# Attention stage of a two-layer gated cross-attention kernel: one power for both norms, aggregate instructions for variances, and a new order of work on every engine

## The chip, the cores and the metric

The kernel runs on one core of one Trainium2 chip. The time is the device time of one execution in microseconds (us). Engines are named as in the profile: PE is TensorE, DVE VectorE, ACT ScalarE, POOL GpSimd, SP the engine that issues the DMAs. Each engine takes its instructions in program order and waits for others by semaphores.

## The reference, cut to what matters

```
x = x + tanh(g_xattn[0]) * retention(layernorm(x), ctx, ctx, Wh, wg, wo, gn_gamma, gn_beta)
x = x + tanh(g_ffn[0]) * bit_ffn(layernorm(x), w1, w2, gamma)
x = x + tanh(g_xattn[1]) * long_conv(ctx, ctx, layernorm(x), ssm_kernel, D, 8)
x = x + tanh(g_ffn[1]) * experts(layernorm(x), ...)

retention:  O = einsum('hst,bthe->bshe', A, V)          # A from scores summed over the batch
            Y = (O - mean) / sqrt(var + 1e-3) * gn_gamma + gn_beta
            return relu(x @ wg) * Y @ wo
layernorm:  (x - mean) / sqrt(var + 1e-5)
bit_ffn:    x = x * rsqrt(mean(x * x) + 1e-6) * gamma
            xq = clip(round(x * s)) / s,  s = 127 / max(max|x|, 1e-5)     # per row, and so for h
            h = gelu(xq @ ternary(w1).T);  return hq @ ternary(w2).T
```

x is 16 x 256 rows of 512; the hidden width of bit_ffn is 2048. The change touches the first two lines' second half: from O to the end of bit_ffn.

## The kernel before

The program has four blocks that run one behind the other: setup, scores (queries, keys, gates and values of all chunks, the sum over the batch, the ternary weights), attention (`attn_block`), and experts. Only `attn_block` changes. It works on 8 chunks (NCH) of 512 rows, each in 4 tiles (j = 0 to 3) of 128 rows. In the text c or q is the chunk.

For a chunk the steps, by the names of the helper functions, are:

- `load_v`, `load_gate`, `load_x` (SP): the chunk's values into `stage`, its gates into `agate`, its rows of x into one of the two halves of `ax`.
- `cut_v` (ACT, then POOL): v into a high and a low part, 2048 columns each.
- `retention(q, s)`, s = 0 and 1 (PE): 24 matmuls of 256 columns into `ps_o`, which has room for one half s; so the next waits for `group_norm` of the one before.
- `group_stats`, `group_shift` (DVE) around `group_pow` (POOL): variance, its power -1/2, the shift; then `group_norm` (ACT) writes `ao`.
- `turn_o(q, k)` (PE): 4 transposes each, into `ps_r` (two banks); `times_gamma` (ACT), `gated` (DVE), `cut_z` (ACT, then POOL): the gated values, in high and low parts.
- `project(q, j)` (PE): 12 matmuls of 512 columns into `ps_r`; `add_x` (DVE) adds x and takes the statistics of x1.
- `pair_variance`, `pair_rms`, `pair_shift` (DVE) with `layer_pow` (POOL), for a pair of tiles: the layer norm's power, then from it the mean square and the power of the rms norm, then scale and shift; `layer_norm` (ACT) writes `ay`, `times_gain` (POOL) multiplies by gamma, `pair_scale` (DVE) takes the maximum and the scales, `round_y` (ACT) and `pair_bf16` (DVE) round to whole numbers in bf16, `turn_y` (SP) is a transposing DMA into `ayqT`.
- `mm1(c, j)` (PE): 4 groups of 4 matmuls of 512 columns, into three banks `ps_h` in turn; `gelu` (ACT) empties a bank; `scale_h` (DVE), `round_h` (ACT), `to_bf16` (DVE): maximum, scale, rounding of h (2048 columns, two buffers); `turn_h` (SP): transposing DMA into `ahqT` (two buffers).
- `mm2(c, j)` (PE): 16 matmuls of 512 columns into the one bank `ps_y`; `residual` (DVE) adds it to x1 and frees the bank; `store` (SP).

All loops over chunks are unrolled in Python. The order on each engine is written out by hand: after a start-up for chunk 0, the body of chunk c runs the ffn half of c (mm1 from tile 1, mm2, gelu, ...) with the retention half of q = c + 1 put between, and ends with mm1(q, 0). `variance` (lines 59 to 70) is six small DVE instructions, called for two columns at a time.

Of the kernel before, what the change touches and what calls it, by code (L numbers as in the profile page):

```python
# [468 lines left out]
def attn_block(nc, ctx, dram, keep):  # L469
# [23 lines left out]
    ostats, omom = sb("aostats", [P, 2, 6]), sb("aomom", [P, 5, 2])  # L493
    ove, orstd, oshift = (sb(n, [P, 2]) for n in ("aove", "aorstd", "aoshift"))
    stats, mom = sb("astats", [P, TJ, 6]), sb("amom", [P, 5, TJ])
    ve, rstd, sq, r2in, r2, scale, shift, amax, qrec, qscale, dq1 = (
        sb("a" + n, [P, TJ]) for n in "ve rstd sq r2in r2 scale shift amax qrec qscale dq1".split())
    hmax, hrec, hscale, dq2 = (sb("a" + n, [P, TJ]) for n in "hmax hrec hscale dq2".split())
# [28 lines left out]

    block = st.enter_context(nc.Block())

    @block.sync  # L530
    def _(sp):
        def load_v(n):
            sp.wait_ge(vlo_done, START + n)
            sp.dma_start(keep["stage"][:], dram["vals"][n]).then_inc(v_in, 16)
# [27 lines left out]
        for n in range(2):  # L562
            if n == 0:
                sp.sem_inc(v_in, 16)
            else:
                load_v(n)
            load_x(n)
            load_gate(n)
        turn_y(0, 0)
        turn_y(0, 1)  # L570
        for c in range(NCH):
            q = c + 1
            if q + 1 < NCH:
                load_v(q + 1)
            turn_h(c, 0)
            store(c, 0)
            if q + 1 < NCH:
                load_gate(q + 1)
            turn_h(c, 1)
            turn_h(c, 2)  # L580
            store(c, 1)
            turn_h(c, 3)
            if q < NCH:
                turn_y(q, 0)
            store(c, 2)
            if q < NCH:
                turn_y(q, 1)
            store(c, 3)
            if q + 1 < NCH:
                load_x(q + 1)  # L590
# [3 lines left out]
    def _(pool):  # L594
# [12 lines left out]
        def layer_pow(q, a):  # L607
            pool.wait_ge(mom_done, 12 * q + 6 * a + 6)
# [15 lines left out]
        cut_v(0)  # L624
        for q in range(NCH):
            if q == 0:
                group_pow(0, 0)
            group_pow(q, 1)
            for k in range(KT):
                cut_z(q, k)  # L630
            if q + 1 < NCH:
                cut_v(q + 1)
# [1308 lines left out]
```

## Time and profile before

| | us |
|---|---|
| three runs | 2332.95, 2332.93, 2327.42 |
| median | 2332.93 |
| profiled execution | 2325.81 |
| its span, first to last instruction | 2324.0 |
| mean granted clock of TensorE | 0.944 |
| busy in the span: PE, DVE, ACT, POOL | 2017.0, 1546.4, 1017.7, 952.0 |

The span is what lies between the first and the last instruction of the profiled execution; its own time is 1.8 us longer. The attention stage begins near 259 us of the span and its last residual starts at 803.31; before it lie setup and scores, behind it the experts. A granted clock of 1 is 2.4 GHz, of 0.5 is 1.2 GHz; a mean between is a mixture of the two. A matmul's record is longer than its spacing from the next, since matmuls overlap in the engine.

### The profile page before, as it was taken

The page shows a single profiled execution, that of the slowest core. Times are in us where ns is not written, and L with a number is a line of the kernel's source. Part 1 is how long each engine was busy: PE and PEld are TensorE (multiplying, and loading weights), DVE is VectorE, ACT ScalarE, POOL GpSimd, SP SyncE. Part 2 cuts the span into 40 slices and gives each one's busy share as a digit, 9 for nine tenths or more (in the row PEclk, how much of TensorE's full clock was granted, in tenths as well). Part 3 has the DMA queues.
Part 4 walks back from the last instruction along what each step waited for, and adds up shares of the span by engine and source line. Part 5 has one row for each costly group of instructions (what it writes and reads, how often), then busy time and mean ns, then how long its engine had stood idle before and what let it go on. Part 6 is the DMA issues. An engine that isn't in the chain of part 4 may idle for free.

```text
span 2324.0 us, 30136 instructions
## 1 busy us (share of the span) xinstructions
PE 2017.0 (87%) x10162; PEld 1602.5 (69%) x10162; DVE 1546.4 (67%) x2487; ACT 1017.7 (44%) x1414; POOL 952.0 (41%) x775
## 2 busy tenths in 40 slices
PE   5999568887787545799899899899899899899998
PEld 4989444444454234688788788788788788688787
DVE  4776456666666358588578678678578579578511
ACT  3345345555555321633633633633633633443432
POOL 0110133333332021465465465465465465365464
PEclk9999779999999857899999999999999999899999
DMA  6666314443443321322332332332232242232231
GB/s 214 235 217 231 131 54 116 111 105 96 108 118 82 69 66 46 104 85 90 111 95 86 109 103 86 106 106 86 93 119 82 80 124 90 72 113 73 69 136 64
DMA packets 169968, 248.76 MB, mean 107 GB/s; under 512 B 91280, under 2 KB 92688, under 8 KB 163632
## 3 DMA queue, kind: packets, MB, share of 16 engines
q1 hardware_dynamic: 169616, 247.86, 34.3%
q8 instruction: 34, 0.56, 0.1%
q14 instruction: 30, 0.25, 0.0%
q10 hardware_dynamic: 288, 0.10, 0.0%
HBM read 193.26 MB, written 33.69 MB: 98 GB/s over the span
## 4 chain that ended last, share of the span: by engine, by line
PE 43%; DVE 7%; issue 6%; ACT 5%; POOL 3%; DMA 1%; ACTq 0%; SPq 0%; DVEq 0%; POOLq 0%
PE e_ps_u L54 4%; PE e_ps_u L56 4%; PE e_ps_u L55 4%; PE e_ps_m L54 4%; PE e_ps_m L56 3%; PE e_ps_m L55 3%; PE e_ps_out L54 3%; PE e_ps_out L55 3%; PE e_ps_out L56 3%; PE e_ps_g L56 3%; PE e_ps_g L55 3%; PE e_ps_g L54 3%; POOL e_dn_lo L1185 1%; DVE e_kv_lo L1504 1%; DVE e_x3T L1532 1%
## 5 line engine op out<-in xcount | busy, mean ns | idle before, releaser
L1180 POOL TENSOR_TENSOR e_gu_lo<-e_gu_raw,e_gu_hi 128x1024 fp32r<-128x1024 f32 (+1 forms) x128 | 272.8, 2131 | 449.6 <-ACT e_gu_hi L1269 447.3
L1532 DVE TENSOR_REDUCE e_x3T<-e_zp 128x128 f32<-128x1024 f32 x128 | 267.4, 2089 | 4.4
L54 PE MATMUL e_ps_u<-e_xn_hi,e_gu_hi 128*128 128x512 f32 x512 | 205.5, 401 | 4.0 <-DVE e_xn_lo L1554 2.5
L54 PE MATMUL e_ps_out<-e_hd_hi,e_dn_hi 128*128 128x512 f32 x512 | 208.8, 408 | 0.0
L54 PE MATMUL e_ps_m<-e_kv_hi,e_t_hi 128*128 128x288 f32 x592 | 180.7, 305 | 29.7 <-DVE e_kv_lo L1504 22.1
L55 PE MATMUL e_ps_out<-e_hd_lo,e_dn_hi 128*128 128x512 f32 x512 | 205.2, 401 | 0.0
L56 PE MATMUL e_ps_out<-e_hd_hi,e_dn_lo 128*128 128x512 f32 x512 | 205.2, 401 | 0.0
L55 PE MATMUL e_ps_u<-e_xn_lo,e_gu_hi 128*128 128x512 f32 x512 | 203.7, 398 | 0.0
L56 PE MATMUL e_ps_u<-e_xn_hi,e_gu_lo 128*128 128x512 f32 x512 | 203.6, 398 | 0.0
L958 PE MATMUL ps_h<-w1q,ayqT 128*128 128x512 bf16 x512 | 130.3, 403 | 79.4 <-ACT ah L681 71.9
L1203 POOL TENSOR_TENSOR e_kv_raw<-e_ke 128x512 f32<-128x512 f32 x128 | 139.4, 1089 | 125.7 <-DVE e_kv_lo L1504 95.5
L1185 POOL TENSOR_TENSOR e_dn_lo<-e_dn_raw,e_dn_hi 128x512 fp32r<-128x512 f32 x128 | 179.6, 1403 | 6.9 <-ACT e_dn_hi L1275 6.9
L1477 DVE TENSOR_TENSOR e_hd_lo<-e_hd,e_hd_hi 128x512 fp32r<-128x512 f32 x128 | 125.2, 978 | 78.6 <-ACT e_hd_hi L1297 78.6
L56 PE MATMUL e_ps_m<-e_kv_hi,e_t_lo 128*128 128x288 f32 x592 | 177.0, 299 | 0.0
L55 PE MATMUL e_ps_m<-e_kv_lo,e_t_hi 128*128 128x288 f32 x592 | 176.8, 299 | 0.0
L1283 ACT ACTIVATE e_sg<-e_ps_g,vecs 128x512 f32<-128x512 f32 x96 | 66.2, 690 | 242.4 <-PE e_ps_g L56 241.5
L1472 DVE SCALAR_TENSOR_TENSOR e_hd<-e_ps_u,vecs,e_sgw 128x512 f32<-128x512 f32 x96 | 71.7, 747 | 140.7 <-PE e_ps_u L56 116.0
L1297 ACT ACTIVATE e_hd_hi<-e_hd 128x512 fp32r<-128x512 f32 x128 | 80.4, 628 | 190.0 <-DVE e_hd L1472 189.7
L1194 POOL TENSOR_TENSOR e_sgw<-e_sg,e_wb 128x512 f32<-128x512 f32 x96 | 127.1, 1324 | 80.2 <-ACT e_sg L1283 79.5
L958 PEld LDWEIGHTS ps_h<-w1q,ayqT 128*128 128x128 bf16 x512 | 48.4, 101 | 151.1 <-ACT ah L681 87.5
L54 PE MATMUL e_ps_g<-e_xn_hi,e_gu_hi 128*128 128x512 f32 x384 | 152.5, 397 | 0.0
L56 PE MATMUL e_ps_g<-e_xn_hi,e_gu_lo 128*128 128x512 f32 x384 | 151.5, 395 | 0.0
(271 smaller groups left out, 5304.7 us busy)
## 6 DMA issues: line engine op xcount, KB each, us to landing
e_gu_raw<-in_mgu SPq DMA_DIRECT2D x96, 512.0 KB, 3.3
e_dn_raw<-in_md SPq DMA_DIRECT2D x128, 256.0 KB, 3.2
e_wb<-wts SPq DMA_DIRECT2D x8, 1536.0 KB, 6.6
stage<-in_x SPq DMA_DIRECT2D x8, 1024.0 KB, 6.8
c<-in_ctxT SPq DMA_DIRECT2D x8, 1024.0 KB, 5.8
raw_w<-in_w1T SPq DMA_DIRECT2D x8, 1024.0 KB, 4.8
raw_w<-in_w2T SPq DMA_DIRECT2D x8, 1024.0 KB, 7.3
gates<-gate SPq DMA_DIRECT2D x8, 1024.0 KB, 4.8
```

Of the source, the lines that this page charges most:

```text
L54: nc.tensor.matmul(out, w_hi, x_hi, start=first, stop=False, skip_group_check=skip)
L55: nc.tensor.matmul(out, w_hi, x_lo, start=False, stop=False, skip_group_check=skip)
L56: return nc.tensor.matmul(out, w_lo, x_hi, start=False, stop=last, skip_group_check=skip)
L958: last = nc.tensor.matmul(h_bank(c, j, n)[:], yqT[:, j, k], keep["w1q"][:, k, n * 512:(n + 1) * 512], start=(k == 0), stop=(k == KT - 1))
L1180: nc.gpsimd.tensor_tensor(gu_lo[:, s % 2, a], gu_raw[:, s % 2, a], f32(gu_hi[:, s % 2, a]), ALU.subtract).then_inc(gulo_done, 1)
L1185: nc.gpsimd.tensor_tensor(dn_lo[:, s % 2], dn_raw[:, s % 2], f32(dn_hi[:, s % 2]), ALU.subtract).then_inc(dnlo_done, 1)
L1194: nc.gpsimd.tensor_tensor(sgw[:], sg[:], wb[:, (s - SHARED) // 2], ALU.mult).then_inc(sgw_done, 1)
L1203: nc.gpsimd.tensor_tensor(out[:, :, 0:32].rearrange("p b (d i) -> p b d i", i=CD), view(ke, m * B * EXT, (EXT, B), (0, 4), (1, CD)), view( ...
L1297: nc.scalar.activation(hd_hi[:, s % 2], hd[:], ACT.Copy).then_inc(hdhi_done, 1)
L1472: nc.vector.scalar_tensor_tensor(out=hd[:], in0=ps_u[:], scalar=vecs[:, V_BU + e:V_BU + e + 1], in1=sgw[:], op0=ALU.add, op1=ALU.mult).the ...
L1477: nc.vector.tensor_tensor(hd_lo[:, s % 2], hd[:], f32(hd_hi[:, s % 2]), ALU.subtract).then_inc(hdlo_done, 1)
L1532: nc.vector.tensor_reduce(x3T[:, lb].rearrange("p (b n) -> p b n", b=B)[:, :, hh * CD:(hh + 1) * CD], zv(5, (1, 8), (21, 8)), AX.X, ALU.ad ...
```

## The change

The norm of x and the rms norm behind it become one power: with v the variance, the scale of both is (v (1 + 1e-6) + 1e-6 * 1e-5) ** -0.5, so `pair_rms`, the second power in `layer_pow` and the product in `pair_shift` go. Variances come from `bn_aggr` (one instruction a tile, mean and variance from the statistics) and one small instruction for the pair, instead of `variance`. In `pair_scale` and `scale_h` a factor 1/127 is merged into the maximum's step, one small instruction less in each.

The hand-written order of all five engines is replaced by a list per engine in which a loop variable i runs over shifted chunks: `at(op, c, ...)` issues the step if chunk c exists. The steps are finer: mm1 and gelu by group n, `layer_norm`, `round_y`, `times_gain` and `to_whole` (formerly `pair_bf16`) by tile. Waits that the old order made needless are added: `group_norm` of s = 0 behind the last chunk's `turn_o`, `layer_norm` behind `to_whole` of the chunk before, `pair_shift` behind its `layer_norm`, `dq1` behind the gelus of the chunk before.

The diff, cut: declarations, semaphore names, the deleted hand-written order (it stands in the listing above) and unchanged steps are left out.

```diff
+    def at(op, c, *which):

+        if 0 <= c < NCH:
+            op(c, *which)
...
+            if n == 0:
+                sp.sem_inc(v_in, 16)
+            else:
+                sp.wait_ge(vlo_done, START + n)
+                sp.dma_start(keep["stage"][:], dram["vals"][n]).then_inc(v_in, 16)
...
+        for i in range(-2, NCH + 2):
+            at(turn_h, i - 2, 2)
+            at(turn_h, i - 2, 3)
+            at(store, i - 2, 0)
+            at(turn_y, i - 1, 1)
+            at(store, i - 2, 1)
+            at(store, i - 2, 2)
+            at(load_x, i)
+            at(store, i - 2, 3)
+            at(turn_h, i - 1, 0)
+            at(load_v, i + 2)
+            at(load_gate, i + 1)
+            at(turn_h, i - 1, 1)
+            at(turn_y, i, 0)
...
-            nc.gpsimd.tensor_tensor(rstd[:, cols], ve[:, cols], mhalf[:, cols], ALU.pow).then_inc(rstd_done, 1)
-            pool.wait_ge(rms_step, 6 * q + 3 * a + 3)
-            nc.gpsimd.tensor_tensor(r2[:, cols], r2in[:, cols], mhalf[:, cols], ALU.pow).then_inc(r2_done, 1)
-
-        def times_gain(q, a):
-            for j in (2 * a, 2 * a + 1):
-                pool.wait_ge(y_done, 4 * q + j + 1)
-                nc.gpsimd.tensor_tensor(y[:, j], y[:, j], keep["gam"][:], ALU.mult).then_inc(yg_done, 1)
+            nc.gpsimd.tensor_tensor(scale[:, cols], ve[:, cols], mhalf[:, cols], ALU.pow).then_inc(scale_done, 1)

+        def times_gain(q, j):
...
+        for i in range(-2, NCH):
+            at(times_gain, i, 2)
+            at(group_pow, i + 1, 1)
+            at(times_gain, i, 3)
+            at(cut_v, i + 2)
+            for k in range(4):
+                at(cut_z, i + 1, k)
+            at(group_pow, i + 2, 0)
+            at(layer_pow, i + 1, 0)
+            at(times_gain, i + 1, 0)
+            at(times_gain, i + 1, 1)
+            at(layer_pow, i + 1, 1)
...
+            if q > 0 and s == 0:
+                act.wait_ge(oT_done, 4 * q)
...
+        def layer_norm(q, j):
+            act.wait_ge(shift_done, 2 * q + j // 2 + 1)
+            if q > 0:
+                act.wait_ge(yq_done, START + 4 * (q - 1) + j + 1)
+            nc.scalar.activation(y[:, j], x1(q)[:, j], ACT.Identity, bias=shift[:, j:j + 1], scale=scale[:, j:j + 1]).then_inc(y_done, 1)

+        def round_y(q, j):
...
+        for i in range(-3, NCH):
+            at(gelu, i, 0, 0)
+            at(group_norm, i + 1, 1)
+            for n in range(1, 4):
+                at(gelu, i, 0, n)
+            at(round_y, i, 2)
+            at(round_y, i, 3)
+            at(times_gamma, i + 1, 0)
+            at(times_gamma, i + 1, 1)
+            at(gelu, i, 1, 0)
+            at(round_h, i, 0)
+            at(cut_z, i + 1, 0)
+            at(times_gamma, i + 1, 2)
+            at(cut_z, i + 1, 1)
+            at(times_gamma, i + 1, 3)
+            at(gelu, i, 1, 1)
+            at(cut_z, i + 1, 2)
+            at(gelu, i, 1, 2)
+            at(cut_z, i + 1, 3)
+            at(gelu, i, 1, 3)
+            for n in range(4):
+                at(gelu, i, 2, n)
+            at(round_h, i, 1)
+            at(round_h, i, 2)
+            at(layer_norm, i + 1, 0)
+            at(layer_norm, i + 1, 1)
+            at(gelu, i, 3, 0)
+            at(group_norm, i + 2, 0)
+            at(gelu, i, 3, 1)
+            at(gelu, i, 3, 2)
+            at(round_y, i + 1, 0)
+            at(round_y, i + 1, 1)
+            at(gelu, i, 3, 3)
+            at(layer_norm, i + 1, 2)
+            at(layer_norm, i + 1, 3)
+            at(cut_v, i + 3)
+            at(round_h, i, 3)
...
-            variance(nc, dve, ostats, omom, ove[:], GN_EPS, omom_done, 12 * q + 6 * s)
+            for b in range(2):
+                nc.vector.bn_aggr(omv[:, b], ostats[:, b]).then_inc(omom_done, 1)
+            dve.wait_ge(omom_done, 6 * q + 3 * s + 2)
+            nc.vector.tensor_scalar(ove[:], omv[:, :, 1], GN_EPS, None, ALU.add).then_inc(omom_done, 1)
...
-            variance(nc, dve, stats[:, cols], mom[:, :, cols], ve[:, cols], LN_EPS, mom_done, 12 * q + 6 * a)
-
-        def pair_rms(q, a):
-
-            cols = slice(2 * a, 2 * a + 2)
-            n = 6 * q + 3 * a
-            dve.wait_ge(rstd_done, 2 * q + a + 1)
-            nc.vector.tensor_tensor(sq[:, cols], rstd[:, cols], rstd[:, cols], ALU.mult).then_inc(rms_step, 1)
-            dve.wait_ge(rms_step, n + 1)
-            nc.vector.scalar_tensor_tensor(out=r2in[:, cols], in0=ve[:, cols], scalar=LN_EPS, in1=sq[:, cols], op0=ALU.subtract,
-                                           op1=ALU.mult).then_inc(rms_step, 1)
-            dve.wait_ge(rms_step, n + 2)
-            nc.vector.tensor_scalar(r2in[:, cols], r2in[:, cols], RMS_EPS, None, ALU.add).then_inc(rms_step, 1)
...
+            for j in (2 * a, 2 * a + 1):
+                nc.vector.bn_aggr(mv[:, j], stats[:, j]).then_inc(mom_done, 1)
+            dve.wait_ge(mom_done, 6 * q + 3 * a + 2)
+            nc.vector.tensor_scalar(ve[:, cols], mv[:, cols, 1], 1.0 + RMS_EPS, RMS_EPS * LN_EPS, ALU.mult, ALU.add).then_inc(mom_done, 1)
...
-            dve.wait_ge(r2_done, 2 * q + a + 1)
-            nc.vector.tensor_tensor(scale[:, cols], rstd[:, cols], r2[:, cols], ALU.mult).then_inc(shift_done, 1)
-            dve.wait_ge(shift_done, 4 * q + 2 * a + 1)
-            nc.vector.scalar_tensor_tensor(out=shift[:, cols], in0=mom[:, 0, cols], scalar=-0.5, in1=scale[:, cols], op0=ALU.mult,
+            dve.wait_ge(scale_done, 2 * q + a + 1)
+            if q > 0:
+                dve.wait_ge(y_done, 4 * (q - 1) + 2 * a + 2)
+            nc.vector.scalar_tensor_tensor(out=shift[:, cols], in0=mv[:, cols, 0], scalar=-1.0, in1=scale[:, cols], op0=ALU.mult,
                                            op1=ALU.mult).then_inc(shift_done, 1)
...
-            nc.vector.tensor_scalar(amax[:, cols], amax[:, cols], 1e-5, None, ALU.max).then_inc(qs_done, 1)
+            nc.vector.tensor_scalar(step[:, cols], amax[:, cols], 1e-5, 1.0 / QMAX, ALU.max, ALU.mult).then_inc(qs_done, 1)
             dve.wait_ge(qs_done, n + 2)
-            nc.vector.reciprocal(qrec[:, cols], amax[:, cols]).then_inc(qs_done, 1)
-            nc.vector.tensor_scalar(dq1[:, cols], amax[:, cols], 1.0 / QMAX, keep["wmean"][:, 0:1], ALU.mult, ALU.mult).then_inc(qs_done, 2)
-            dve.wait_ge(qs_done, n + 5)
-            nc.vector.tensor_scalar(qscale[:, cols], qrec[:, cols], QMAX, None, ALU.mult).then_inc(qs_done, 1)
...
-            nc.vector.tensor_scalar(hmax[:, col], hmax[:, col], 1e-5, None, ALU.max).then_inc(hs_done, 1)
+            nc.vector.tensor_scalar(hstep[:, col], hmax[:, col], 1e-5, 1.0 / QMAX, ALU.max, ALU.mult).then_inc(hs_done, 1)
             dve.wait_ge(hs_done, n + 2)
-            nc.vector.reciprocal(hrec[:, col], hmax[:, col]).then_inc(hs_done, 1)
-            nc.vector.tensor_scalar(dq2[:, col], hmax[:, col], dq2w[:], None, ALU.mult).then_inc(hs_done, 1)
-            dve.wait_ge(hs_done, n + 4)
-            nc.vector.tensor_scalar(hscale[:, col], hrec[:, col], QMAX, None, ALU.mult).then_inc(hs_done, 1)
+            nc.vector.reciprocal(hscale[:, col], hstep[:, col]).then_inc(hs_done, 1)
+            nc.vector.tensor_scalar(dq2[:, col], hstep[:, col], dq2w[:], None, ALU.mult).then_inc(hs_done, 1)
...
+        for i in range(-2, NCH + 1):
+            at(pair_variance, i, 1)
+            at(residual, i - 1, 0)
+            at(to_whole, i, 0)
+            at(to_whole, i, 1)
+            at(pair_shift, i, 1)
+            at(scale_h, i - 1, 3)
+            at(group_stats, i + 1, 1)
+            at(residual, i - 1, 1)
+            at(group_shift, i + 1, 1)
+            at(to_bf16, i - 1, 3)
+            at(pair_scale, i, 1)
+            at(scale_h, i, 0)
+            at(residual, i - 1, 2)
+            at(gated, i + 1, 0)
+            at(to_whole, i, 2)
+            at(to_whole, i, 3)
+            at(gated, i + 1, 1)
+            at(to_bf16, i, 0)
+            at(gated, i + 1, 2)
+            at(gated, i + 1, 3)
+            at(residual, i - 1, 3)
+            at(group_stats, i + 2, 0)
+            at(scale_h, i, 1)
+            at(scale_h, i, 2)
+            at(add_x, i + 1, 0)
+            at(add_x, i + 1, 1)
+            at(group_shift, i + 2, 0)
+            at(pair_variance, i + 1, 0)
+            at(to_bf16, i, 1)
+            at(pair_shift, i + 1, 0)
+            at(to_bf16, i, 2)
+            at(add_x, i + 1, 2)
+            at(add_x, i + 1, 3)
+            at(pair_scale, i + 1, 0)
...
-                pe.wait_ge(x1_done, START + 4 * q)
+                pe.wait_ge(x1_done, START + 4 * q - 1 + k)
...
+        for i in range(-2, NCH + 1):
+            at(mm2, i - 1, 1)
+            for n in range(4):
+                at(mm1, i, 0, n)
+            at(mm2, i - 1, 2)
+            at(turn_o, i + 1, 0)
+            at(turn_o, i + 1, 1)
+            for n in range(3):
+                at(mm1, i, 1, n)
+            at(turn_o, i + 1, 2)
+            at(turn_o, i + 1, 3)
+            at(mm2, i - 1, 3)
+            at(retention, i + 2, 0)
+            at(mm1, i, 1, 3)
+            for n in range(4):
+                at(mm1, i, 2, n)
+            at(project, i + 1, 0)
+            at(project, i + 1, 1)
+            at(mm1, i, 3, 0)
+            at(mm1, i, 3, 1)
+            at(project, i + 1, 2)
+            at(project, i + 1, 3)
+            at(mm1, i, 3, 2)
+            at(mm2, i, 0)
+            at(mm1, i, 3, 3)
+            at(retention, i + 2, 1)
```

## Rows read from the trace of the kernel before

**Rows 1.** Windows view: span, length, busy of PE, PEld, DVE, ACT, POOL, clock.
```profile
546.00:607.00 61.00, 49.23 (x243) 29.79 (x242) 41.11 (x94) 33.20 (x41) 19.28 (x15) 0.97 0.43 112
...
900.00:1000.00 100.00, 70.05 (x349) 58.22 (x350) 64.45 (x110) 44.76 (x66) 36.26 (x33) 0.80 0.25 77
```

**Rows 2.** Waits in the attention stage (329 to 803): total, times, longest.
```profile
PE ps_h L958 <- ACT ah L681: 71.9, 31, 6.0
...
PE ps_y L966 <- DVE ax L843: 20.8, 15, 3.9
```

**Rows 3.** Timeline of TensorE (start, length): where mm1 of chunks 0, 1, 7 begins.
```profile
318.23 5.30 PE L958 MATMUL ps_h<-w1q,ayqT 128*128 128x512 bf16 x12 [7.25 <-DMA ayqT<-ayq]
...
386.60 2.75 PE L958 MATMUL ps_h<-w1q,ayqT 128*128 128x512 bf16 x12
...
756.36 2.75 PE L958 MATMUL ps_h<-w1q,ayqT 128*128 128x512 bf16 x12
```

**Rows 4.** Timeline of TensorE: matmuls of the four kinds at the full clock.
```profile
301.14 0.39 PE L54 MATMUL ps_r<-wo_hi,az_hi 128*128 128x512 f32 x1
...
307.94 0.28 PE L54 MATMUL ps_o<-av_hi,at_hi 128*128 128x256 f32 x1
...
310.70 0.28 PE L56 MATMUL ps_o<-av_hi,at_lo 128*128 128x256 f32 x1
...
346.61 3.62 PE L966 MATMUL ps_y<-w2q,ahqT 128*128 128x512 bf16 x16
...
350.06 2.75 PE L958 MATMUL ps_h<-w1q,ayqT 128*128 128x512 bf16 x12
```

**Rows 5.** Groups by line, 424.96 to 485.87: count, busy us, mean ns.
```profile
L681 ACT ACTIVATE ah<-ps_h,adq 128x512 f32<-128x512 f32 x16 | 10.2, 685 | 3.6 <-PE ps_h L958 3.5
...
L822 DVE TENSOR_REDUCE ahmax<-ah 128x1 f32<-128x2048 f32 x4 | 9.1, 2281 | 1.3 <-ACT ah L681 1.3
...
L686 ACT ACTIVATE ah<-ah,arnd,ahscale 128x2048 f32<-128x2048 f32 x4 | 8.3, 2087 | 0.0
...
L767 DVE SCALAR_TENSOR_TENSOR ax<-ps_r,gains,ax 128x512 f32<-128x512 f32 x5 | 3.7, 748 | 14.6 <-PE ps_r L56 14.5
```

**Rows 6.** Timeline of VectorE in the first chunk, the chain to the shift.
```profile
304.22 0.16 DVE L62 TENSOR_TENSOR amom<-astats 128x2 f32<-128x2 f32 x1
...
305.80 0.16 DVE L782 TENSOR_TENSOR asq<-arstd 128x2 f32<-128x2 f32 x1 [0.81 <-POOL arstd L610]
...
307.17 0.16 DVE L792 TENSOR_TENSOR ascale<-arstd,ar 128x2 f32<-128x2 f32 x1 [0.81 <-POOL ar L612]
...
311.03 1.22 DVE L802 TENSOR_REDUCE aamax<-ay 128x2 f32<-128x1024 f32 x1 [3.50 <-POOL ay L617]
```

**Rows 7.** Timeline of VectorE and GpSimd where both are at work.
```profile
446.85 2.50 POOL L617 TENSOR_TENSOR ay<-ay,gam 128x512 f32<-128x512 f32 x2 [1.32 <-ACT ay L670]
...
447.16 0.97 DVE L62 TENSOR_TENSOR aomom<-aostats 128x2 f32<-128x2 f32 x1
...
477.12 1.50 DVE L837 TENSOR_SCALAR ahq<-ah 128x2048 bf16<-128x2048 f32 x1
...
477.89 5.11 POOL L597 TENSOR_TENSOR av_lo<-stage,av_hi 128x2048 fp32r<-128x2048 f32 x1 [0.36 <-ACT av_hi L645]
```

**Rows 8.** Timeline where the stage starts and ends.
```profile
294.25 0.80 PE L54 MATMUL ps_r<-wo_hi,az_hi 128*128 128x512 f32 x1 [5.40 <-POOL az_lo L605]
...
785.06 1.89 PE L958 MATMUL ps_h<-w1q,ayqT 128*128 128x512 bf16 x4 [3.91 <-ACT ah L681]
...
803.31 0.75 DVE L843 SCALAR_TENSOR_TENSOR ax<-ps_y,adq,ax 128x512 f32<-128x512 f32 x1 [4.12 <-PE ps_y L966]
```

**Rows 9.** DMA issues 329 to 800: line, count, KB each, median us to landing.
```profile
ax<-in_x SPq DMA_DIRECT2D x6, 1024.0 KB, 5.7
...
ahqT<-ahq SPq DMA_TRANSPOSE x32, 4.3
...
ayqT<-ayq SPq DMA_TRANSPOSE x15, 3.1
```

More of the change, by code:

```diff
@@ L561, in _ @@
         sp.sem_inc(x2_out, START)
[L562 to L590, printed above, removed]
+        for i in range(-2, NCH + 2):
[12 more added lines that the diff above has]
+            at(turn_y, i, 0)
         sp.wait_ge(x2_out, START + 16 * TJ * NCH)
@@ L623, in _ @@
         pool.wait_ge(consts_done, 1)
[L624 to L632, printed above, removed]
-            for a in range(2):
-                layer_pow(q, a)
-                times_gain(q, a)
-            if q + 1 < NCH:
-                group_pow(q + 1, 0)
+        for i in range(-2, NCH):
[10 more added lines that the diff above has]
+            at(layer_pow, i + 1, 1)
     @block.scalar
@@ L808, in pair_scale @@
[L808 to L816 removed]
+            nc.vector.reciprocal(qscale[:, cols], step[:, cols]).then_inc(qs_done, 1)
@@ L949, in project, with mm1 @@
             last.then_inc(wo_done, 1)
-        def mm1(c, j):
-            pe.wait_ge(yT_in[j // 2], 16 * (c + 1))
-            for n in range(4):
-                if 16 * c + 4 * j + n >= HBANKS:
-                    pe.wait_ge(gelu_done, START + 16 * c + 4 * j + n - HBANKS + 1)
-                for k in range(KT):
-                    last = nc.tensor.matmul(h_bank(c, j, n)[:], yqT[:, j, k], keep["w1q"][:, k, n * 512:(n + 1) * 512],
-                                            start=(k == 0), stop=(k == KT - 1))
-                last.then_inc(h_done, 1)
+        def mm1(c, j, n):
+            if n == 0:
+                pe.wait_ge(yT_in[j // 2], 16 * (c + 1))
+            if 16 * c + 4 * j + n >= HBANKS:
+                pe.wait_ge(gelu_done, START + 16 * c + 4 * j + n - HBANKS + 1)
+            for k in range(KT):
+                last = nc.tensor.matmul(h_bank(c, j, n)[:], yqT[:, j, k], keep["w1q"][:, k, n * 512:(n + 1) * 512],
+                                        start=(k == 0), stop=(k == KT - 1))
+            last.then_inc(h_done, 1)
         def mm2(c, j):
@@ L969, in _ @@
         pe.sem_inc(mm2_done, START)
-        retention(0, 0)
-        retention(0, 1)
-        for k in range(KT):
-            turn_o(0, k)
-        for j in range(TJ):
-            project(0, j)
-        retention(1, 0)
-        mm1(0, 0)
-        for c in range(NCH):
-            q = c + 1
-            last = q == NCH
-            if not last:
-                retention(q, 1)
-            mm1(c, 1)
-            mm1(c, 2)
-            if not last:
-                for k in range(KT):
-                    turn_o(q, k)
-            mm2(c, 0)
-            mm1(c, 3)
-            if not last:
-                for j in range(TJ):
-                    project(q, j)
-            mm2(c, 1)
-            if q + 1 < NCH:
-                retention(q + 1, 0)
-            mm2(c, 2)
-            mm2(c, 3)
-            if not last:
-                mm1(q, 0)
+        for i in range(-2, NCH + 1):
[24 more added lines that the diff above has]
+            at(retention, i + 2, 1)
     st.close()
```

172 lines of the change are left out of this document (30 added, 142 removed).

## Prediction, made before the changed kernel was run

> **What bounds the kernel now.** I read five views, in this order. The busy time in windows of about one chunk (61 us) says which engine is nearest to its limit: TensorE is busy 49.2 us of 61, VectorE 41.1, ScalarE 33.2, GpSimd 19.3, at a granted clock of 0.97 [rows 1]. So no engine is full, and the time of the attention stage is made by waits. The view of who waited for whom, over the stage, says which: TensorE's first-layer matmuls `ps_h` stand 71.9 us behind ScalarE's gelu and its second-layer matmuls 20.8 us behind the residual (there is one bank `ps_y`) [rows 2]. A program in a fixed order on five queues waits in one place because the order of another puts something in front. The timeline of TensorE gives the length of a round, counted from mm1(c, 0) to mm1(c+1, 0): 318.23 to 386.60, 68.4 us, for the first, then (756.36 - 386.60) / 6 = 61.6, and 62.6 over all seven [rows 3]. The stage is some 545 of the 2324 us of the span; the setup and scores before it and the experts behind it (there the granted clock and the busy time are another matter [rows 1]) are not touched, and I carry them over unchanged.
>
> **What TensorE alone needs for a round.** At the full clock, 16 second-layer matmuls start 350.06 - 346.61 = 3.45 us after the 16 before, 0.216 each; mm1 has the same shape. 64 + 64 of them make 27.6. The projection's matmuls start (307.94 - 301.14) / 30 = 0.227 apart, 48 make 10.9; retention's (310.70 - 307.94) / 23 = 0.12, 48 make 5.8 [rows 4]. The 16 transposes at about that last rate make 1.9. The sum is 46.2 us. So a new order can take at most 62.6 - 46.2 = 16.4 from a round, times 7 = 115 us. The small arithmetic is not worth much by itself; whether that floor is reached is the question.
>
> **Small operations.** In the first chunk nothing hides the chain from the statistics to the shift: six variance steps and a power take 305.80 - 304.22 = 1.58 us, three steps and a second power 307.17 - 305.80 = 1.37, then two steps; a step is 0.16 busy [rows 6]. The change drops the second power with its three steps (1.37) and the product `scale` (0.2), and turns six variance steps into three (two bn_aggr, one add). No row shows a bn_aggr. Three small steps are 0.5 against at most 1.0 for six; from above, an instruction over 512 columns takes 0.75 [rows 5], and one over 6 no more: 2 x 0.75 + 0.16 = 1.66. So the variance moves by -0.5 to +0.7; I take -0.3, as a 6-column step is nearest to the small ones. The chain shortens by about 1.9 us, twice per chunk. VectorE loses 26 small instructions per chunk (24 variance steps become 12, six rms steps and two products go, six scalings are merged), 26 x 0.16 = 4.2: 41.1 - 4.2 = 37 us busy. GpSimd loses two powers of at most 1.37 - 3 x 0.16 = 0.9: 17.6 or more [rows 1, 6].
>
> **The new order, walked.** I put TensorE's new list at its floor, with 0 at mm2(i-1,1), and ask of each other engine whether it delivers in time, with durations from [rows 5]: gelu 0.69 (0.6 when they follow each other, the records overlap), round_h 2.09, cut_v as round_h (as many columns), scale_h 2.28 for the maximum and 0.4 for its steps, add_x 0.75 with 0.7 of statistics, to_bf16 1.2 (1.50 with a hold in it [rows 7]), other 512-column work 0.75.
> TensorE: mm2(i-1,1) 0 to 3.5, mm1(i,0) to 6.9, mm2(i-1,2) to 10.4, turn_o 0 and 1 to 11.4, mm1(i,1) three quarters to 14.0, turn_o 2 and 3 to 15.0, mm2(i-1,3) to 18.5, retention(i+2,0) to 21.4, mm1 to 25.7, project 0 and 1 to 31.1, mm1 to 32.8, project 2 and 3 to 38.3, mm1 39.1, mm2(i,0) 42.6, mm1 43.5, retention(i+2,1) 46.2.
> Then: gelu(i,2,3) ends at 26.5; scale_h(i,2) to 29.3; add_x 0 and 1 to 33.3; add_x 3 ends 40.0; pair_scale 41.7; round_y 43.1; residual(i,0) has to wait for mm2(i,0), 43.5; to_whole 44.3; the transpose of y lands 3.1 later [rows 9], at 47.5. mm1(i+1,0) is due at 46.2 + 3.5 = 49.7, so 2.2 us are spare. The same tail, from the maximum to the first matmul, took 318.23 - 311.03 = 7.2 us where nothing stood in it [rows 3, 6]; here it has 40.0 to 49.7. The late gelu(i,3,3), the cut of v behind retention(i+2,1), and round_h(i-1,3) end at 4.2 of the next round, and gelu(i,0,0) is due for mm1(i,0,3) at 6.0, spare about 1. The transposes of h land in 4.3 [rows 9] with over 10 us to spare in three cases of four; h(i-1,3) is the tight one, below.
> DMAs are queued on SP in the list's order. load_x(i+1) waits for residual(i-1,3), at about 22, and holds back store(i-1,3), turn_h(i,0) (due 39), load_v, load_gate and turn_h(i,1). The load lands in 5.7 [rows 9], at 28 to 29, and add_x(i+1,0) wants it at 29.3: just in time. If it is late, VectorE is held by the excess and project 2 still has some 3 us.
> So by the engines' order alone TensorE would hardly stop.
>
> **What the walk must add: GpSimd and VectorE in each other's way.** From 446.85 GpSimd multiplies two tiles in 2.50; a two-column add on VectorE, begun at 447.16, takes 0.97 instead of 0.16, until 448.13, when the first of the two is through. At 477.12 a to_bf16 begins and ends at 478.62; GpSimd's part of cut_v, begun at 477.89, takes 5.11, of which 4.4 lie behind that end [rows 7]. Before, cut_v fell where VectorE waited for the projection. The new lists put it (and times_gain 3) right behind group_pow, and VectorE then has group_shift (two inputs from SBUF), to_bf16(i-1,3) and pair_scale before it. group_shift at 4.4 gets in before cut_v at 4.6; to_bf16 then stands from 4.8 to about 9.4, pair_scale ends at 12.2 instead of 7.5, and round_y 2 and 3 hold ScalarE's times_gamma until 13.6. turn_o 2 starts at 14.4 instead of 14.0, and residual(i-1,2) and h(i-1,3)'s transpose come at 15.5 for an mm2 due at 15.0. From there VectorE catches up, waiting again for project 3. So a hold by cut_v is 4.4 to 5.1 long. It costs 4.6 us of VectorE and some 0.7 of TensorE. Between 0 (the waiting is hidden) and 4.6 (all of it reaches TensorE) I take 0.7. With 1.6 for ordinary lateness (load_x, handoffs, some matmuls at half clock after a gap) I set a round at 46.2 + 0.7 + 1.6 = **48.5 us**.
> The Trainium skill, page SBUF — State Buffer, section Who interferes with whom, says that VectorE with two SBUF inputs, or in a two-port mode, and GpSimd exclude each other for a whole instruction, whichever came first. By that rule the group_shift too stands 4.5 us if cut_v is first, so it speaks against this order, and the rival B below is what it would give. The trace agrees in the 0.97 us row.
>
> **Start and end.** Before the first round the new list puts retention(1,0) into the 5.4 us in which TensorE waited for `az_lo` [rows 8]. It is off the path, and the projection starts at the full clock: 14 matmuls save 0.2 each, 2.8. With the 1.9 of the chain that is 4.7. Against it, cut_v(1) now follows group_pow(0,1) on GpSimd directly, and group_shift(0,1) may stand for its 4.5 us. Bounds 0 and 4.5; I take half. So mm1(0,0) starts 2.4 earlier, at 315.8. The first round has the start-up in it: 51 instead of 68.4. At the end, from mm1(7,0) on, before took 803.31 + 0.75 - 756.36 = 47.7 [rows 3, 8]. The last gelu, scale, rounding, transpose, mm2 and residual, from the end of the last mm1 at 785.06 + 1.89, take 804.1 - 787.0 = 17 in both [rows 8]. In the new list the last mm1 is reached about 24.5 after mm1(7,0), so 41.5: 6 less.
>
> **The sum.** mm1(7,0) starts at 315.8 + 51 + 6 x 48.5 = 657.8 instead of 756.4: 98.6 less. With 6 at the end it is 105 less than the profiled execution of 2325.8, that is 2221. The median of the runs shown lies 7 us above that execution; I take half of this, 2224.
>
> **Rivals.**
> A, the floor: the waits vanish, rounds of 46.2 (49 the first), mm1(0,0) at 313.6. 313.6 + 49 + 277.2 = 639.8, 123 less with the end: 2203. It counts into the forecast and gives its low end.
> B, the holds are not absorbed: VectorE stands behind cut_v for 4.5 us and TensorE with it, each round. 48.5 + 4.5 = 53, 7 x 4.5 = 31 more: 2255. For it: the 0.97 us row [rows 7], and cut_v's place. Against it: VectorE has 46.2 - 37 = 9 us of room. Its far end is VectorE and GpSimd never at work together: 37 + 17.6 = 55 a round, 7 x (62.6 - 55) = 53 and 8 at the ends less, 2265 to 2272.
> C, the order changes nothing, and only the shorter chain counts: twice 1.9 per round, 7 x 3.8 = 27 and 8 at the ends: 2291 to 2298. The waits of TensorE for gelu [rows 2] would stay at 70 us. Against it: these waits are made by what the old list puts between gelus, and that is what is moved.
> D, slower: TensorE's waits become many and short instead of few, and the granted clock falls. In the window 900 to 1000 the clock is 0.80 with TensorE busy 70 us of 100 [rows 1], against 0.97 in the stage. The place is all of TensorE's list. A round then takes 46.2 / clock + 2.3; it passes 62.6 + 1.2 (what the ends save, per round) from a clock of 0.75 down, and at 0.70 it is 68.3, giving 2326 + 7 x 5.7 - 8 = 2358. Against it: the walk leaves no gap of more than about 1 us.
> E, none of it measurable: rounds of 62, 2320 to 2333.
>
> **Chances.** Forecast with A 0.67 (rounds of 46 to 51 us, 2200 to 2245), B 0.22, C 0.06, E 0.02, D 0.03. A range of 2200 to 2266 holds the first and nearly all of B. A measurement of this kernel can tell about 0.3% (7 us) from no change. Faster by more than that: 0.95; within 0.02; slower 0.03.
>
> **What would show it.** Right: mm1(c,0) starts 48 to 49 us apart; `ps_h` behind gelu falls from 71.9 to under 15; TensorE's clock at 0.98 or more; VectorE 37 busy per round; bn_aggr at 0.2 or less; mm1(0,0) near 316; 41 us from mm1(7,0) to the end. Wrong: to_bf16 or group_shift of 2 to 5 us beside cut_v in every round together with TensorE idle at mm2(·,3) or turn_o (B); waits of add_x for x; a landing of the y transpose over 5 us; a clock below 0.9 (D).

## The result and the profile after

| | before | after |
|---|---|---|
| median, us | 2332.66 | 2190.18 |
| lowest and highest of four runs | 2327.42, 2332.95 | 2189.53, 2191.32 |
| profiled execution | 2325.81 | 2189.84 |
| its span | 2324.0 | 2188.0 |
| last residual ends | 804.06 | 674.16 |
| from there to the end of the span | 1519.9 | 1513.8 |

The ratio after/before is 0.9395, with a 95% interval of 0.9378 to 0.9411. The change is faster, by 142 us; 2224 was forecast, and 2190.2 lies below the low end of the range, 2200.

The windows of the changed kernel (span, length, busy of PE, PEld, DVE, ACT, POOL with their instructions, granted clock, DMA share, GB/s) answer [rows 1]:

```profile
409.00:456.00 47.00, 47.00 (x246) 29.47 (x245) 41.30 (x70) 34.68 (x43) 21.69 (x14) 1.00 0.58 146
...
546.00:607.00 61.00, 61.00 (x319) 36.79 (x318) 52.92 (x87) 45.15 (x60) 24.67 (x16) 1.00 0.51 121
```

TensorE is busy 47.00 us of 47 and 61.00 of 61, at the full clock: in this stage it has become the bound. VectorE is busy 41.30 us of 47, which is 40.5 in a round of 46.1 and not 37 as forecast. The largest waits of TensorE from 320 to 660 answer [rows 2]:

```profile
PE ps_h L902 <- ACT ah L668: 2.2, 3, 1.2
PE ps_y L910 <- DMA ahqT<-ahq: 1.9, 1, 1.9
```

Of the 71.9 us behind gelu 2.2 are left. Of the 20.8 behind the residual none is left up to 660 and 0.8 in the last pass behind it. Now it is ScalarE that waits for TensorE: the same view for all engines has `ACT ah L668 <- PE ps_h L902: 24.0, 53, 2.2`. The timeline of TensorE has these starts of mm1 for chunks 0, 1, 6 and 7, against [rows 3]:

```profile
316.89 5.04 PE L902 MATMUL ps_h<-w1q,ayqT 128*128 128x512 bf16 x16 [4.83 <-DMA ayqT<-ayq]
...
361.07 0.59 PE L902 MATMUL ps_h<-w1q,ayqT 128*128 128x512 bf16 x2
...
591.64 0.38 PE L902 MATMUL ps_h<-w1q,ayqT 128*128 128x512 bf16 x1
...
632.92 0.60 PE L902 MATMUL ps_h<-w1q,ayqT 128*128 128x512 bf16 x2 [0.33 <-DMA ayqT<-ayq]
```

The first round takes 44.2 us (68.4 before), the next five (591.64 - 361.07) / 5 = 46.1 each (61.6), the last 41.3. The floor of the prediction was 46.2. From mm1(7,0) to the last residual, which starts at 673.41 and takes 0.75, it is 41.2 (47.7 before, [rows 8]).

VectorE in the first chunk, and then VectorE and GpSimd in a steady round, answer [rows 6] and [rows 7]:

```profile
304.57 0.25 DVE L757 BATCH_NORM_AGGREGATE amv<-astats 128x2 f32<-128x6 f32 x2
...
305.83 0.16 DVE L766 SCALAR_TENSOR_TENSOR ashift<-amv,ascale 128x2 f32<-128x2 f32 x1 [0.81 <-POOL ascale L602]
...
454.38 1.22 DVE L806 TENSOR_SCALAR ahq<-ah 128x2048 bf16<-128x2048 f32 x1
454.40 5.58 POOL L589 TENSOR_TENSOR av_lo<-stage,av_hi 128x2048 fp32r<-128x2048 f32 x1
...
456.75 3.25 DVE L776 TENSOR_SCALAR astep<-aamax 128x2 f32<-128x2 f32 x1
```

Two bn_aggr take 0.25 us together. The chain from the statistics to the shift's start is 305.83 - 304.57 = 1.3 us, against 304.22 to 307.37 before, so 1.9 shorter, as worked out. And GpSimd's part of cut_v does hold VectorE in each of the five rounds from 361 to 592: it is a scaling of two columns that stands 3.25 us for its usual 0.17. to_bf16, which was expected to be held, began 0.02 us ahead of cut_v and ran in 1.22, and it was cut_v that took 5.58 (4.5 where nothing stands in its way).

### The profile page after: what moved, and what is told of

Its sections match the earlier page's. It is cut to its first block, busy times and chain, and to the rows that moved or that the text cites. A ratio compares the mean times of both kernels' runs of the same rounds, so it can differ in the third digit from the quotient of the medians.

```text
span 2188.0 us, 30039 instructions
## 1 busy us (share of the span) xinstructions
PE 1979.3 (90%) x10162; PEld 1588.5 (73%) x10162; DVE 1541.2 (70%) x2279; ACT 1021.4 (47%) x1414; POOL 960.0 (44%) x759
## 4 chain that ended last, share of the span: by engine, by line
PE 45%; DVE 7%; issue 6%; ACT 5%; POOL 3%; DMA 1%; ACTq 0%; SPq 0%; DVEq 0%; POOLq 0%
PE e_ps_u L54 4%; PE e_ps_u L55 4%; PE e_ps_u L56 4%; PE e_ps_m L54 4%; PE e_ps_m L56 3%; PE e_ps_m L55 3%; PE e_ps_out L54 3%; PE e_ps_out L56 3%; PE e_ps_out L55 3%; PE e_ps_g L56 3%; PE e_ps_g L54 3%; PE e_ps_g L55 3%; POOL e_dn_lo L1124 1%; DVE e_kv_lo L1443 1%; DVE e_x3T L1471 1%
## 5 line engine op out<-in xcount | busy, mean ns | idle before, releaser
L55 PE MATMUL e_ps_g<-e_xn_lo,e_gu_hi 128*128 128x512 f32 x384 | 151.4, 394 | 0.0
L54 PEld LDWEIGHTS e_ps_m<-e_kv_hi,e_t_hi 128*128 128x128 f32 x592 | 113.0, 191 | 48.9 <-DVE e_kv_lo L1443 17.1
```

The source lines that it names most:

```text
L54: nc.tensor.matmul(out, w_hi, x_hi, start=first, stop=False, skip_group_check=skip)
L55: nc.tensor.matmul(out, w_hi, x_lo, start=False, stop=False, skip_group_check=skip)
```

## The experiments

Times are medians; "rounds" are the steady ones in the middle of the stage, from the starts of gelu(c,0,0).

### The new order alone, the new arithmetic alone

```diff
+            at(pair_rms, i, 1)
             at(pair_shift, i, 1)
...
+            at(pair_rms, i + 1, 0)
             at(pair_shift, i + 1, 0)
```

That is VectorE's new list with the old `variance`, two powers and separate scalings.

> The new lists on every engine with the old arithmetic (six-step variances, two powers and the three steps between, the separate scalings). Theory 1, the order alone did it and TensorE at its floor hides the arithmetic: mm1(c,0) starts stay 46.1 us apart, the start-up before mm1(0,0) grows by 1 to 3 us, and the time is 2190 to 2197 us. Rival, the shorter arithmetic was needed: VectorE was busy 41.3 us of a 46.1 us round in the changed kernel, of which some 5 stood behind GpSimd; with 26 small instructions more (4.2) it would be the bound, rounds of 48 us or more and 2203 us or more.

Measured: 2212.97, ratio 0.9503 (0.9487 to 0.9519), rounds of 48.4. The other half is the old order with the aggregates, one power and merged scalings:

> The old order with the new arithmetic. If the chain from the statistics to the shift is on the path in each round (rival C of the prediction), it takes 3.8 us from each of seven rounds and some 2 at the start: 2300 to 2306 us. If other waits stand behind it and take its place, the rounds stay near 61.6 us and the time is 2322 to 2332 us.

Measured: 2300.75, ratio 0.9879 (0.9863 to 0.9896), rounds of 58.0 instead of 61.6. That is 3.6 us per round, close to the 3.8 that rival C put on the shorter chain. The order alone brings 116.6 us, the arithmetic alone 28.8, both 142.5. In the kernel with the new order alone, the largest wait of TensorE from 370 to 600 and the window of that stretch:

```profile
PE ps_r L896 <- ACT az L649: 6.9, 5, 1.4
```

```profile
370.00:600.00 230.00, 221.19 (x1117) 137.16 (x1135) 212.75 (x437) 158.91 (x196) 107.69 (x71) 1.00 0.56 141
```

With the old arithmetic VectorE is busy 212.75 us of 230, and TensorE waits once a round, for ScalarE's times_gamma. In the kernel with the new arithmetic alone the first of TensorE's waits from 329 to 790 is `PE ps_h L945 <- ACT ah L678: 54.5, 30, 4.4`: in the old order the waits for gelu remain, 54.5 of 71.9 us.

### One piece of the old order

```diff
             round_h(c, 1)
-            if q + 1 < NCH:
-                cut_v(q + 1)
             round_h(c, 2)
             gelu(c, 3)
+            if q + 1 < NCH:
+                cut_v(q + 1)
```

> The kernel before with one step of ScalarE moved: cut_v of the next chunk behind the gelus of tile 3 instead of in front of them. In the kernel before TensorE waits 4.39 us in each round for the first of these gelus. If ScalarE's order makes the waits, each round loses cut_v's 1.9 us, 6 x 1.9 = 11 us, and the time is 2319 to 2323 us. Rival: the wait only moves (to layer_norm behind ashift, or to the projection) and the time stays within 3 us of the kernel before.

Measured: 2331.82, ratio 1.0012 (1.0003 to 1.0022): no gain, 0.1% longer if anything. From 329 to 803 the wait for gelu fell from 71.9 to 68.5 us, that for the residual rose from 20.8 to 26.9. Moving this step alone only moves the wait; what the new order gains is not in it. No other step was moved by itself, so which steps of the new lists bring the gain is not shown.

### The cut of v held back

In these runs GpSimd's part of cut_v waits until VectorE is through with what it would hold. First for chunk 1 alone:

```diff
             pool.wait_ge(vhi_done, q + 1)
+            if q == 1:
+                pool.wait_ge(oshift_done, 2)
```

> The changed kernel with one wait more: GpSimd begins the second cut_v only when VectorE's second group_shift is through. If that step stood 4.3 us behind GpSimd for the shared access to SBUF and was on the path, mm1(0,0) starts 4 us earlier (312.6 to 313.5 us instead of 316.9) and the time is 2185 to 2187 us. Rival: cut_v then stands in the way of the gated and cut_z steps that follow, and mm1(0,0) stays at 316 to 317 us.

Measured: 2188.70, ratio 0.9397 (0.9381 to 0.9412). The 4.45 us of group_shift(0,1) are 0.16 again, but mm1(0,0) starts only at 316.04. In this run group_stats(0,1) started 2.05 later than in the changed kernel's (281.37 against 279.32), so from there on 2.9 of 4.3 us are gained. Of the rest 0.8 goes to `gated`, 2.24 for a pair that now lies beside cut_v, 1.47 before. Then, with this wait kept, in every round:

```diff
+            if q > 1:
+                pool.wait_ge(qs_done, 8 * (q - 1))
```

> The changed kernel in which GpSimd begins each cut_v only when the VectorE steps that it would hold are through: the second group_shift in the first chunk, pair_scale of tiles 2 and 3 in each round. If the holds are absorbed in the steady rounds but not at the start, rounds stay at 46.1 us while VectorE's busy time falls from 41.3 to about 38, the first round (44.2 us from mm1(0,0) to mm1(1,0)) shortens by 1 to 3 us, and the time is 2184 to 2187 us. Rival: cut_v now holds gated instead and cut_z comes late for the projection, rounds of 47 us or more, 2195 us or more.

Measured: 2187.30 (2186.26 to 2192.72), ratio 0.9390 (0.9373 to 0.9407). By these intervals the total is not clear of the changed kernel's; the starts in the traces are. mm1(0,0) starts at 313.86, from group_stats(0,1) at 279.22: 34.6 us, and 37.6 in the changed kernel. The timeline of a steady round:

```profile
453.61 0.21 DVE L785 TENSOR_SCALAR adq<-astep,wmean 128x2 f32<-128x2 f32 x1
454.79 2.29 DVE L798 TENSOR_REDUCE ahmax<-ah 128x1 f32<-128x2048 f32 x1 [0.97 <-ACT ah L672]
457.11 0.15 DVE L800 TENSOR_SCALAR ahstep<-ahmax 128x1 f32<-128x1 f32 x1
457.49 0.74 DVE L816 SCALAR_TENSOR_TENSOR ax<-ps_y,adq,ax 128x512 f32<-128x512 f32 x1
...
453.96 4.54 POOL L593 TENSOR_TENSOR av_lo<-stage,av_hi 128x2048 fp32r<-128x2048 f32 x1 [2.95 <-DVE adq L785]
```

Nothing of VectorE's is held: from 453.96 to 458.50 it runs a maximum, one-column scalings and a residual from `ps_y` at their usual lengths, and `gated` begins 0.2 before the end. It is busy 187.46 us from 370 to 600 instead of 200.50: 37.6 in a round of 46.1, the 37 of the prediction. And the rounds are 46.1 as before. So in the changed kernel the hold costs nothing in a steady round: VectorE had the time. At the start, where TensorE waits for that chain, it costs 2.9.

### How much room VectorE has

A reduction over 2048 columns is done once more per round on VectorE, ahead of pair_scale(i+1, 0), and in a second kernel twice (`range(2)`); the result is not used.

```diff
+        def extra(c):
+            for n in range(1):
+                nc.vector.tensor_reduce(load[:, c, n:n + 1], keep["w1q"][:, n], AX.X, ALU.add)
```

> The changed kernel with idle work added on VectorE: in each round one sum over 2048 columns of the weights, into a scratch column that nobody reads, just in front of the second last step (pair_scale of tiles 0 and 1), on the way from the projection to the next mm1(c,0). It should take 2.2 to 2.3 us. Theory 1, the walk was right that 2.2 us are spare on this way: rounds stay at 46.1 to 46.4 us and the time at 2190 to 2193. Rival, the way has no room and VectorE's idle time of 4.8 us a round lies elsewhere: rounds of 48.3 us, 2204 us.

> The same with two such sums in each round, 4.4 to 4.6 us. Theory 1 (2.2 us spare): rounds longer by 2.2 to 2.4 us, 48.4, and 2204 to 2208 us. Rival 1 (no room): rounds of 50.6 us, 2222 us. Rival 2 (all of VectorE's idle 4.8 us can be used up): rounds stay at 46.1 to 46.5, 2190 to 2194 us.

Measured: 2200.01, ratio 0.9432 (0.9416 to 0.9447), rounds of 46.8; and 2218.10, ratio 0.9513 (0.9497 to 0.9529), rounds of 49.0. The first 2.27 us cost 0.7 a round, both together (4.46) cost 2.9: about 1.5 are free, where the walk had 2.2 at the transpose of y. The times rise by 9.8 and 27.9 us, of which the five steady rounds are 3.6 and 14.6. The rest lies before the first of them and in the last two passes: from mm1(7,0) to the end of the stage it is 44.8 and 46.1 us instead of 41.2, with a sum in that pass too. So a delay of five us on that path would not be hidden, though VectorE idles for 5.9 us in a round; the hold, 3 us long, fell where it was harmless.

### Holds twice as long

GpSimd's part of cut_v is done twice in a row.

```diff
+            nc.gpsimd.tensor_tensor(v_lo[:], v, f32(v_hi[:]), ALU.subtract).then_inc(twice, 1)
+            pool.wait_ge(twice, q + 1)
```

> The changed kernel with GpSimd's part of cut_v done twice, so that VectorE's two-column scaling step, which stood 3.25 us behind it, stands 4.5 us longer. Theory 1 (the walk: the step leads through round_y and times_gamma to turn_o 2, where TensorE arrives 1.3 us later than it must; the trace of the changed kernel shows about that room): rounds of 49 us, 2209 us. Rival B of the prediction (a hold reaches TensorE in full): 50.6 us, 2222 us. Rival (holds vanish in VectorE's idle time of 4.8 us): 46.1 us, 2190 us.

Measured: 2228.66, ratio 0.9557 (0.9541 to 0.9573), rounds of 51.2, more than either theory gave. The timeline shows one hold for each of the two:

```profile
478.29 3.25 DVE L779 TENSOR_SCALAR astep<-aamax 128x2 f32<-128x2 f32 x1
...
481.65 4.47 DVE L784 TENSOR_SCALAR adq<-astep,wmean 128x2 f32<-128x2 f32 x1
...
475.93 5.58 POOL L590 TENSOR_TENSOR av_lo<-stage,av_hi 128x2048 fp32r<-128x2048 f32 x1
481.59 4.51 POOL L592 TENSOR_TENSOR av_lo<-stage,av_hi 128x2048 fp32r<-128x2048 f32 x1
```

Whether the 5.1 us per round are the hold or GpSimd's own lateness, the same two cuts held back as above tell:

> All work of the changed kernel; GpSimd's cut of v is done twice, as in the run that lost 5.1 us per round, but both only after VectorE has written the scales of the pair before them. Theory 1 (the 5.1 us were VectorE standing behind the cut for twice its length): VectorE is only touched where it has little left to do before it waits for the projection, rounds 46.1 to 47.5, time 2187 to 2198. Theory 2 (the 5.1 us were GpSimd's own lateness: cut_z and the powers behind a cut of twice the length): the second cut now ends some 4 us later still, so rounds of 51 or more, time 2228 or more.

Measured: 2204.61, ratio 0.9461 (0.9443 to 0.9479), rounds of 47.1. Twice the work of GpSimd costs 1.0 us per round behind pair_scale and 5.1 ahead of it, although behind it GpSimd is later still: its second cut ends 13.4 us after residual(i-1,1) starts, and 11.1 when it runs ahead. So four fifths of it hang on where VectorE stands. (In the total it is 17.3 and 38.5 us. Much of the 17.3 lies ahead of the first round: mm1(0,0) starts at 324.08 for 313.86, and already the first retention, behind the first doubled cut, starts at 270.70 for 265.18.) (The second cut still holds a pair of to_whole here, 6.18 us for 0.75; this lies in the remaining 1.0.) Rival B is a real mechanism, and the changed kernel is short of the point from which it decides: the first hold costs nothing, the second, 4.3 us more on VectorE, nearly all of its length, 4.1 of the 5.1. (The granted clock there is 0.96 instead of 1.00 from 370 to 600, so a part may be the clock's.)

### Why the arithmetic is worth 23 us in the new order

> All work is done, with the old small arithmetic (two powers, six-step variances, separate scalings) in the new order, and GpSimd's cut of v held back until VectorE has written the scales of the pair before it (so that it no longer stands over to_bf16 and pair_scale). Theory 1 (in the new order VectorE is the bound once the old arithmetic is in it, 45 of 48.5 us busy, and some 5 of those 45 are it standing for GpSimd's cut of v, counted as busy): with the hold gone VectorE is 41 to 42 busy of a round, rounds fall from 48.4 to 46.5 to 47.5, time 2196 to 2205. Theory 2 (the 23 us that the arithmetic is worth in the new order are its chain of small steps and powers between engines, not VectorE's room): rounds stay at 48 or more, time 2209 to 2216. Price of a round: 7 of them, so 1 us in a round is 6 to 7 us in the time.

Measured: 2198.80, ratio 0.9438 (0.9421 to 0.9455), rounds of 46.6, VectorE busy 210.68 of 230. Here the edit is the one that holds every cut back, with 12 for 8 (the old scalings raise `qs_done` six times per pair), in the kernel with the new order alone. Holding the cut back brings 2213.0 - 2198.8 = 14.2 us with the old arithmetic and 2190.2 - 2187.3 = 2.9 with the new. With the cut held back in both, the arithmetic is worth 2198.8 - 2187.3 = 11.5, without it 22.8. The two compete for the same room on VectorE: the hold alone is absorbed, the old arithmetic alone costs 0.5 us a round, both together 2.3. Of the 11.5 us that remain with the cut held back, the rounds are thus some 3; in the profiled executions mm1(0,0) starts 5.4 later with the old arithmetic (319.26 for 313.86), 1.8 of it because group_stats(0,1) does (281.00 for 279.22), the rest in the chain, which nothing hides there.

### The six microseconds behind the stage

Behind the stage the code is the same, yet it takes 6.1 us less. Measured from the end of the last residual, the maxima `e_x3T` of the experts start within 3.4 us of each other in both kernels up to the 96th (984.1 and 983.2 us); between the 112th and the 113th the kernel before loses 5.4 us (77.6 against 72.2). ScalarE's timeline there, before:

```profile
2020.64 0.59 ACT L1361 ACTIVATE e_sgw<-e_ps_g 16x512 f32<-16x512 f32 x1 [4.59 <-issue]
```

and after:

```profile
1885.79 0.59 ACT L1300 ACTIVATE e_sgw<-e_ps_g 16x512 f32<-16x512 f32 x1 [0.31 <-PE e_ps_g L1711]
```

ScalarE stands 4.59 us and waits for nothing that the profile shows. The same stand is in all three profiled kernels with the old lists (4.52 to 4.59) and in none of the nine with the new ones, and of the eight `e_sgw` it is at the seventh only. Copies of one column into a tile that nobody reads were put ahead of the stage on ScalarE in the kernel before, 36 of them as shown and 12 in a second kernel:

```diff
+        for k in range(36):
+            nc.scalar.activation(scrap[:, k:k + 1], keep["vecs"][:, V_BETA:V_BETA + 1], ACT.Copy)
         cut_v(0)
```

> The kernel before, with 12 one-column copies into a tile that nobody reads added on ScalarE ahead of the attention stage (where ScalarE waits for the first retention); all work is done. Asked is why ScalarE stands 4.6 us with nothing shown ahead of its copy into e_sgw in the kernels with the old lists and not in those with the new ones. Theory 1 (it depends on where that instruction lies in ScalarE's program, so the count of instructions ahead of it decides): with 12 more ahead of it, the 4.6 us at e_sgw are gone or at another instruction. Theory 2 (it comes from the work around it, the same in each kernel with the old lists): still 4.5 to 4.6 us at e_sgw. Time 2325 to 2334 by theory 2, 5 less where theory 1 makes it vanish.

> As the run with 12 copies, with 36. Theory 1 (the place in ScalarE's program decides): the 4.6 us at e_sgw are gone or at another instruction, not necessarily as with 12. Theory 2 (the work around it decides): still 4.5 to 4.6 us at e_sgw, time 2325 to 2334.

Measured, one run each: 2330.15 with 12, where the stand is still there, at the same instruction (4.56); 2327.14 with 36, where it is gone:

```profile
2022.90 0.59 ACT L1364 ACTIVATE e_sgw<-e_ps_g 16x512 f32<-16x512 f32 x1 [0.31 <-PE e_ps_g L1775]
```

With 36 the time behind the stage is 1514.3, as in the kernels with the new lists (1513.7 to 1515.5); in the four with the stand it is 1519.9 to 1525.9, a spread that is not the stand's. Between the 112th and the 113th maximum it takes 72.4 us with 36, 77.4 with 12. The work around the instruction is the same, only the count of instructions ahead of it on ScalarE differs, so its place in ScalarE's program decides; that 12 do not move it and 36 do says that this is coarse.

VectorE has such stands too, and the changed kernel has one:

```profile
1895.67 0.19 DVE L1520 TENSOR_TENSOR e_ew<-e_ew,e_keepw 128x32 f32<-128x32 f32 x1 [4.40 <-issue]
```

It is at this instruction, 4.29 to 4.54 us long, in all five kernels with the changed kernel's list for VectorE, and in none of the four new-order kernels in which that list has more instructions. There it costs nothing that the maxima show (72.2 us between the 112th and the 113th with it and without it). In the kernel with the new arithmetic alone VectorE stands 4.13 us at `e_zp` besides ScalarE's 4.52, and that stretch takes 81.9 us instead of 77.6: its 28.8 us are net of this, and in the stage itself the arithmetic brings 804.06 - 772.27 = 31.8.

What the engine waits for is not among the semaphores, but the DMA view has a trace of it. From 1035 to 2016 of the kernel before, the queue `q14 instruction` moves nothing; from 2016 to 2021, where ScalarE stands, the view has

```profile
q14 instruction: 1, 0.01, 0.4%
```

and the same line stands for the changed kernel from 1891 to 1896, where VectorE stands, and none from 860 to 1891. With 36 copies there is no such packet from 1035 to 2086. A wait for a piece of the engine's program fits all of this; the view does not say for which engine a packet is, so it is not shown.

## Why the prediction was wrong, by its own steps

The direction, the bound and the mechanism held; the size did not. The sum of the prediction, 2221, is 31.2 above the profiled 2189.84. Two terms were mis-sized, what was added to the floor and the first and last rounds. By terms:

- **What was added to the floor**: 0.7 for the hold and 1.6 for "ordinary lateness". Five rounds ran at 46.1 instead of 48.5: 12 us. This is the first step that failed. The walk had found spare time of 1 to 2 us at each tight place, and lateness smaller than the spare time costs nothing: a queue's delay is not added to the bound's time, it is first taken from the slack. The 0.7 was got from the same walk, but for a hold of to_bf16 that did not come. The one that came stood over pair_scale, 3.25 us a round, and the run with every cut held back puts its price at 0.0.
- **The first and the last round**, the second step that failed: the last was counted like the others, 48.5, but the list for i = 6 has no retentions, 2 x 2.88 us, and nothing came of the 2.3 for lateness and hold; it took 41.3, 7.2 us less. The first was put at 51 for its start-up, but it lacks mm2(-1,2) and mm2(-1,3), 2 x 3.45 us. By the list it needs 39.3 at the full clock, and with 2.1 us of waits and a granted clock of 0.97 it took 44.2: 6.8 us less. What is missing in both could be read from the lists.
- **mm1(0,0)** started at 316.9, not 315.8. group_shift(0,1) was held for its whole 4.45 us (from 281.92, cut_v from 281.85), not half of it; that cost 2.9 on the path, as the held-back run shows with 313.86 from a group_stats(0,1) that starts 0.10 earlier. The prediction took half of its bounds 0 and 4.5. The rule it had named (the Trainium skill, SBUF — State Buffer, section Who interferes with whom) has the later of the two stand for the whole instruction, and this step did.
- **The end**: 41.2 against 41.5.
- **Behind the stage**: 6.1 less, where the prediction carried it over unchanged. 5.4 of it fall where one stand of ScalarE, 4.59 long, was removed by chance.

Together 12 + 7.2 + 6.8 - 1.1 + 0.3 + 6.1 = 31.3. The 3 us added for the median's offset were wrong as well: of the four runs of the changed kernel the highest lies 1.5 us above the profiled one.

What held: the floor (46.2 against 46.1), the small operations (two bn_aggr in 0.25, chain 1.9 shorter, VectorE at 37 once the hold is taken off), the granted clock at 1.00 in the stage (rival D), C's price of the arithmetic (28.8 us measured alone, 31.8 in the stage, 28 to 35 forecast), and landings of [rows 9] that hardly changed (x 6.3 us, h 4.3, y 3.3). Rival A, the floor, is what came in the rounds, and the time went below even its 2203. It got no chance of its own and gave the low end, though it too counted the ends too long and the rest unchanged. A low end is not held by the floor of the steady rounds alone: what can still be shorter are the ends, and code that is not touched.

## What to carry over

Once a floor of the bound engine and a hand walk both say that each wait has slack, forecast the floor, and price lateness only where it is longer than the slack; then count the first and the last pass from the lists themselves. Small arithmetic is worth its time on the path in an order that waits for it, and mostly its room on the engine in one that doesn't: here 29 us in the old order, 23 in the new and 11 once the hold is out of the way. A step of GpSimd goes behind VectorE's small steps on the critical chain, or ahead of them by its whole length.

## What the runs showed of the hardware

**Holds.** Beside GpSimd's subtraction of two SBUF tiles, a two-column tensor_scalar of VectorE took 3.25 and 4.47 us instead of 0.17 and 0.21, and a two-column scalar_tensor_tensor from SBUF 4.45 instead of 0.16. A one-column tensor_scalar (0.15), a maximum over 2048 (2.29) and a residual with one input in PSUM (0.74) were not held. Where a to_bf16 of VectorE and a cut of GpSimd began within 0.02 us of each other, in five rounds, VectorE was first each time and took its usual 1.22, and the cut took 5.58 instead of 4.5. The Trainium skill, page SBUF — State Buffer, section Who interferes with whom, gives this split: two SBUF inputs or a two-port mode exclude GpSimd for a whole instruction, at most one input without such a mode does not. The runs agree; that two columns are enough for it was not expected.

**A stand without a wait.** ScalarE stood 4.5 to 4.6 us at one instruction, 1200 us behind the changed stage, by its place in the program, and VectorE 4.1 to 4.5 at others. In each of these ten stands lies a packet of the queue `q14 instruction`; that the engine waited for it is not shown. Here an untouched block moved by 5 us when the count of instructions ahead of it changed.
